# One Mamba-style decoder layer: powers behind other key chunks on GpSimd, squares summed with ones stationary, keys loaded ahead of weights

## The chip, the cores and the metric

The kernel runs on one core of one Trainium2 chip. The metric is the device time of one execution in microseconds, the median of several runs. A core has TensorE (PE, matmuls, with its weight loads listed apart as PEld), VectorE (DVE), ScalarE (ACT), GpSimd (POOL), and SyncE (SP), whose queue issues the DMAs.

## What is computed

The layer works on x of 8 batches x 128 positions x 512 channels in float32. Cut to what matters here:

```python
# 1: state-space mixer, 128 heads of 64, 8 groups of 16 heads
y = Y * silu(gate)                             # 8192 channels
gg = y.reshape(b, s, 8, 1024)
gg = gg * rsqrt(mean(gg * gg, axis=-1) + EPS)  # a root mean square of each group
x = layernorm(x + (gg * norm_w) @ out_proj_w.T)
# 2: attention over ctx: 32 query heads of 16, 8 key heads, 128 keys, no projections
x = layernorm(x + softmax(q @ k.T / 4 + mask) @ v)
# 3: feed-forward, 1792 hidden
x = layernorm(x + (silu(x @ Wg.T) * (x @ Wu.T)) @ Wd.T)
```

## The kernel before

All batches stay on chip. Each engine has its own program written out by hand, and semaphores tie them together: `wait_ge(S["name"], n)` holds an engine until the count is there, `then_inc` raises it.

**Mixer.** 64 tiles of 128 channels (two heads each; `TILES`), eight tiles a group (`TPG`), go through in 72 steps. For a tile, TensorE projects (lines 249 to 251: float32 as high and low parts in three matmuls of 512 columns), ScalarE and VectorE do convolution and decay, TensorE makes the head outputs (`outputs`, line 1216, into `ps_y`), VectorE combines and gates them (`combine`), and ScalarE copies them as `g_hi` (line 603) and squares them into `sq_tmp` (line 606). GpSimd adds the squares of the group's tiles into `sq_acc` (`add_square`). Output products (`out_products`, lines 1224 to 1226) are made of four tiles at a time (`TPH`).

**End of the mixer.** The last group has its own order. TensorE's part starts after the loop: `last_products` for batches 0 to 3 on the tiles that are ready, the outputs of tile 63, `earlier_squares` (sums of `sq_acc` over the 128 channels, eight matmuls with one moving column, line 1286), `last_squares` (the same for the two halves of `sq_tmp` of tile 63, line 1295), then the other products: batches 0 to 3 in `ps_hs` and `ps_gate`, 4 and 5 in `ps_dec`, 6 and 7 in `ps_gate` again. VectorE takes the two sums (lines 1010 and 1016), ScalarE the root, VectorE the reciprocal (line 816). Then for each batch VectorE adds the group's first half (`first_part`, line 810, two SBUF inputs) and its second half (`second_part`, line 1001, from PSUM), and takes the statistics of the first layernorm (`row_stats`, lines 968 and 970). Groups before the last sum their squares on another path (`square_sums`, `group_variance`: ones stationary, 512 columns, and the diagonal taken by a reduce against the identity, line 876).

**Attention.** 32 key chunks, four a batch. For chunk i GpSimd spreads the keys into a block-diagonal tile `k_bd` (line 506; two buffers, so it waits for the scores of chunk i-2), TensorE makes the scores (`scores`, line 1386, two matmuls of 64 rows), VectorE adds the mask and takes the minimum in eight reduces (`masked`, line 1048), ScalarE takes eight exponentials (line 715), TensorE turns the result (line 1396), ScalarE and VectorE each copy a half (`keep_turned`, lines 723 and 1057), and TensorE multiplies by the values (line 1410) and turns back. The layernorm's power -0.5 is taken by GpSimd (`powers`, lines 498 and 501) between two chunks. Its loop:

```python
for i in range(CHUNKS):
    need(pool, S["s_ps"], 2 * i - 2)
    gp.tensor_tensor(k_bd[i % 2][:, :, :],
...
    if i == 3:
        powers(1, slice(2, HB))
```

VectorE normalises (`normed`, line 986) batches 2 and 3 after the first powers, 4 to 7 after the second, and for the next stage 0 to 3 after the third, from chunk 23 on.

**Feed-forward.** It starts in the attention's last chunks, when batches 0 to 3 are ready (line 1439), and is a dense stream of matmuls.

**SyncE's queue** at the end of the mixer: mask, keys (`k_rep`, two loads from HBM, then six copies inside SBUF, line 346), values, then `w_gate` and `w_up` (lines 349, 350; 1.75 MB each), then `w_down` in tiles.

## Time and profile before

| what | us |
|---|---|
| median of 3 runs | 1640.75 |
| lowest, highest | 1639.96, 1640.96 |
| profiled execution: its own time | 1639.42 |
| profiled execution: span | 1637.7 |

| engine | busy us | share of the span | instructions |
|---|---|---|---|
| TensorE, matmuls | 1612.5 | 98% | 9120 |
| TensorE, weight loads | 1271.7 | 78% | 9120 |
| VectorE | 1193.1 | 73% | 2355 |
| GpSimd | 976.6 | 60% | 741 |
| ScalarE | 946.3 | 58% | 1578 |

The mixer takes the span to about 1366 us, the attention from there to about 1477, the feed-forward the rest. The shares are means over these three parts. An f32 matmul whose operands are not split by the program leaves two records in the trace, one for each pass.

### The profile page before, as it was taken

Reading aid. Unit: us, or ns where it says so; the run is one execution under the profiler, and the core shown is the slowest. Engines: PE = TensorE matmul, PEld = TensorE weight load, DVE = VectorE, ACT = ScalarE, POOL = GpSimd, SP = SyncE. Lnnn points to the kernel's source line nnn. Section 1 sums busy time; section 2 is a strip of 40 time slices with the busy share of each in tenths; the row PEclk is TensorE's granted clock in tenths of the full one; section 3 lists DMA queues with packets and bytes.
Section 4 is the critical chain, followed back from the end, with each engine's and each line's share of the span. In section 5 each row is a group of like instructions: output and inputs, shape, how many; then the busy total and the mean of one; then the engine's idle time right before and its main releaser. Section 6 shows DMA issues by size and latency. Waiting matters only on the chain.

```text
span 1637.7 us, 25607 instructions
## 1 busy us (share of the span) xinstructions
PE 1612.5 (98%) x9120; PEld 1271.7 (78%) x9120; DVE 1193.1 (73%) x2355; ACT 946.3 (58%) x1578; POOL 976.6 (60%) x741
## 2 busy tenths in 40 slices
PE   9999999999999999999999999999999998989998
PEld 7788888888888888888888888888888885544646
DVE  7767687767877686868685868586858689996433
ACT  6765377446745583648373837383738375985231
POOL 4977478656956694759484959385938573331000
PEclk9999999999999999999999999999999999999999
DMA  5422134213312241224231413141413254000000
GB/s 202 146 103 82 55 109 130 78 59 102 129 61 84 90 136 57 92 68 132 73 103 50 143 59 123 46 136 58 136 45 115 80 99 116 1 18 23 13 14 26
DMA packets 73571, 138.85 MB, mean 85 GB/s; under 512 B 6786, under 2 KB 10882, under 8 KB 73092
## 3 DMA queue, kind: packets, MB, share of 16 engines
q1 hardware_dynamic: 73444, 137.21, 26.5%
q8 instruction: 73, 1.20, 0.3%
q14 instruction: 54, 0.44, 0.1%
HBM read 132.98 MB, written 2.63 MB: 83 GB/s over the span
## 4 chain that ended last, share of the span: by engine, by line
PE 92%; DVE 4%; issue 1%; POOL 1%; DMA 1%; ACT 1%; SPq 0%; DVEq 0%; POOLq 0%; ACTq 0%
PE ps_hs L249 8%; PE ps_hs L251 8%; PE ps_hs L250 8%; PE ps_gate L250 8%; PE ps_gate L249 8%; PE ps_gate L251 8%; PE ps_y L1216 7%; PE ps_hs L1224 7%; PE ps_hs L1226 7%; PE ps_hs L1225 7%; PE ps_gate L1200 4%; PE ps_y L1514 3%; PE ps_hs L1439 3%; PE ps_dec L1439 3%; DVE pr L1048 2%
## 5 line engine op out<-in xcount | busy, mean ns | idle before, releaser
L798 DVE SCALAR_TENSOR_TENSOR conv<-ps_hs,cw,conv 128x508 f32<-128x508 f32 (+2 forms) x432 | 320.0, 741 | 31.6 <-ACT conv L565 20.4
L399 POOL TENSOR_TENSOR cum_bc<-cum_bc,neg_cum 128x1024 f32<-128x1024 f32 x128 | 247.4, 1932 | 10.8 <-POOL cum_bc L389 0.2
L249 PE MATMUL ps_hs<-x_hi,w_hi 128*128 128x512 f32 x576 | 231.3, 402 | 0.0
L251 PE MATMUL ps_hs<-x_hi,w_lo 128*128 128x512 f32 x576 | 225.1, 391 | 0.0
L249 PE MATMUL ps_gate<-x_hi,w_hi 128*128 128x512 f32 x576 | 224.2, 389 | 0.0
L250 PE MATMUL ps_hs<-x_lo,w_hi 128*128 128x512 f32 x576 | 224.2, 389 | 0.0
L250 PE MATMUL ps_gate<-x_lo,w_hi 128*128 128x512 f32 x576 | 224.1, 389 | 0.0
L251 PE MATMUL ps_gate<-x_hi,w_lo 128*128 128x512 f32 x576 | 224.0, 389 | 0.0
L1224 PE MATMUL ps_hs<-wo_hi,g_hi 128*128 128x512 f32 x488 | 190.4, 390 | 0.0
L1226 PE MATMUL ps_hs<-wo_hi,g_lo 128*128 128x512 f32 x488 | 190.2, 390 | 0.0
L1225 PE MATMUL ps_hs<-wo_lo,g_hi 128*128 128x512 f32 x488 | 190.1, 390 | 0.0
L833 DVE TENSOR_TENSOR m_sb<-ps_dec,cb 128x512 f32<-128x512 f32 x256 | 174.0, 680 | 12.7 <-ACT ps_dec L598 12.6
L603 ACT ACTIVATE g_hi<-ps_y 128x512 fp32r<-128x512 f32 x128 | 75.4, 589 | 178.9 <-DVE ps_y L845 178.7
L372 POOL TENSOR_TENSOR w_lo<-w_raw,w_hi 128x1024 fp32r<-128x1024 f32 (+1 forms) x72 | 172.2, 2392 | 8.1 <-ACT w_hi L529 2.4
L598 ACT ACT_TABLE_LOAD x64 | 82.1, 1283 | 160.3 <-DVE cb L805 159.3
L598 ACT ACTIVATE ps_dec<-cum_bc 128x512 f32<-128x512 f32 x256 | 149.5, 600 | 35.8 <-DVE m_sb L833 30.3
L389 POOL TENSOR_SCALAR_AFFINE_SELECT cum_bc<-cum_bc 128x1024 f32<-128x1024 f32 x128 | 140.5, 1098 | 31.7 <-DMA cum_bc<-cum_scratch 30.7
L565 ACT ACTIVATE conv<-ps_hs,cbias,cw 128x512 f32<-128x512 f32 x144 | 112.7, 783 | 65.6 <-PE ps_hs L251 65.5
L411 POOL TENSOR_TENSOR sq_acc<-sq_acc,sq_tmp 128x512 f32<-128x512 f32 x110 | 140.8, 1299 | 9.2 <-ACT sq_tmp L606 9.2
L841 DVE SCALAR_TENSOR_TENSOR ps_y<-hs,d_col,ps_y 128x512 f32<-128x512 f32 x128 | 95.9, 749 | 62.3 <-PE ps_y L1216 62.3
L469 POOL CAST wo_hi<-wo_sc 128x512 fp32r<-128x512 f32 x64 | 39.2, 612 | 152.8 <-PE ps_hs L1226 152.7
L1216 PEld LDWEIGHTS ps_y<-m_sb,xdt 128*64 128x64 f32 x2048 | 110.7, 137 | 25.1 <-issue 23.7
(176 smaller groups left out, 3334.2 us busy)
## 6 DMA issues: line engine op xcount, KB each, us to landing
cum_bc<-cum_scratch SPq DMA_DIRECT2D x128, 512.0 KB, 4.1
w_raw<-w_in SPq DMA_DIRECT2D x145, 256.0 KB, 4.6
wo_raw<-w_out SPq DMA_DIRECT2D x64, 256.0 KB, 5.0
g_acc<-x_t SPq DMA_DIRECT2D x4, 512.0 KB, 6.2
acc<-x_nat SPq DMA_DIRECT2D x1, 2048.0 KB, 9.7
out<-y_out SPq DMA_DIRECT2D x8, 256.0 KB, 2.0
wg_sb<-w_gate SPq DMA_DIRECT2D x1, 1792.0 KB, 13.6
wu_sb<-w_up SPq DMA_DIRECT2D x1, 1792.0 KB, 15.3
```

The source lines that it names most:

```text
L249: eng.matmul(ps, whi, xhi, start=(k == 0), stop=False)
L250: eng.matmul(ps, whi, xlo, start=False, stop=False)
L251: return eng.matmul(ps, wlo, xhi, start=False, stop=(k == n - 1))
L372: return gp.tensor_tensor(w_lo[slot][:, subs], w_raw[slot][:, subs], w_hi[slot][:, subs].bitcast(F32), ALU.subtract)
L399: gp.tensor_tensor(part, part, start.broadcast_to([P, 2, HB, SEQ]), ALU.add).then_inc(S["bc_ok"], 1)
L598: sc.activation(ps_dec[e][:, :], cum_bc[bh][:, e, :], ACT.Exp).then_inc(S["exp_ok"], 1)
L798: v.scalar_tensor_tensor(out=dst, in0=src, scalar=cw[:, at, TAPS - 1 - n:TAPS - n], in1=dst, op0=ALU.mult, op1=ALU.add).then_inc(S["tap"], 1)
L833: v.tensor_tensor(flat(m_sb[:, q]), ps_dec[q % 2][:, :], flat(half(cb, q // 2)), ALU.mult)\
L1216: mm = pe.matmul(ps_y[bh][e * HD:(e + 1) * HD, b * SEQ:(b + 1) * SEQ], xdt[:, bh * HB + b, e * HD:(e + 1) * HD], m_sb[:, 2 * bh + e, b, :] ...
L1224: pe.matmul(ps, g_hi[:, j, cols], wo_hi[:, j, :], start=(j == 0), stop=False)
L1225: pe.matmul(ps, g_hi[:, j, cols], wo_lo[:, j, :], start=False, stop=False)
L1226: return pe.matmul(ps, g_lo[:, j, cols], wo_hi[:, j, :], start=False, stop=(j == TPH - 1))
```

## The change

Three pieces. On GpSimd the three `powers` move behind later chunks of keys: from 3, 7 and 23 to 4, 9 and 25. In the last group the squares are summed with `ones` stationary and 512 squares moving, four matmuls that accumulate in the two `ps_dec` banks, in place of sixteen with one moving column; every row of a bank then holds all sums, and VectorE takes the diagonal in eight reduces against `ident`. The third matmul waits only for the first half of the squares of tile 63, and both groups now stand ahead of all products of tiles 62 and 63. SyncE waits for the six key copies ahead of the two feed-forward weights.

```diff
@@ SyncE
             sp.wait_ge(S["exp_ok"], 4 * TILES)
+            sp.wait_ge(S["k_in"], 16 * 2 * REP)
             sp.dma_start(wg_sb[:, :, :], w_gate).then_inc(S["wg_in"], 16)
@@ GpSimd
-                if i == 3:
+                if i == 4:
                     powers(1, slice(2, HB))
-                if i == 7:
+                if i == 9:
                     powers(1, slice(HB, BATCH))
-                if i == 23:
+                if i == 25:
                     powers(2, slice(0, HB))
@@ VectorE
-            dve.wait_ge(S["ss_early"], 1)
-            v.tensor_scalar(rstd_g[:, :], ps_dec[0][:, 0:BATCH], 1.0 / (TPG * P), EPS, ALU.mult, ALU.add)\
-                .then_inc(S["ss_part"], 1)
             dve.wait_ge(S["m3_in"], 16)
             v.tensor_scalar(mask_sb[:, :], mask_sb[:, :], -1.0, None, ALU.mult).then_inc(S["m3_neg"], 1)
-            dve.wait_ge(S["ss_part"], 1)
-            dve.wait_ge(S["ss_ps"], GROUPS)
-            v.scalar_tensor_tensor(out=rstd_g[:, :], in0=ps_y[0][:, 0:BATCH], scalar=1.0 / (TPG * P),
-                                   in1=rstd_g[:, :], op0=ALU.mult, op1=ALU.add).then_inc(S["rstd_v"], 1)
+            for b in range(BATCH):
+                cols = slice(b % HB * SEQ, (b % HB + 1) * SEQ)
+                if b % HB == 0:
+                    dve.wait_ge(S["ss_half"], b // HB + 1)
+                v.tensor_tensor_reduce(out=sq_tmp[:, b // HB, cols], in0=ps_dec[b // HB][:, cols], in1=ident[:, :],
+                                       scale=1.0, scalar=0.0, op0=ALU.mult, op1=ALU.add,
+                                       accum_out=rstd_g[:, b:b + 1]).then_inc(S["ss_diag"], 1)
+            dve.wait_ge(S["ss_diag"], BATCH * GROUPS)
+            v.tensor_scalar(rstd_g[:, :], rstd_g[:, :], 1.0 / (TPG * P), EPS, ALU.mult, ALU.add)\
+                .then_inc(S["rstd_v"], 1)
@@ TensorE
             def earlier_squares(t):
                 pe.wait_ge(S["sq_add"], 2 * t)
-                for b in range(BATCH):
-                    mm = pe.matmul(ps_dec[0][:, b:b + 1], sq_acc[:, b * SEQ:(b + 1) * SEQ], ones[:, 0:1],
-                                   start=True, stop=True)
-                mm.then_inc(S["ss_early"], 1)
+                pe.wait_ge(S["m_ok"], 4 * t + 4)
+                for h in range(2):
+                    pe.matmul(ps_dec[h][:, :], ones[:, :], sq_acc[:, h * HALF:(h + 1) * HALF], start=True, stop=False)
             def last_squares(t):
-                pe.wait_ge(S["sq_ok"], 2 * t + 2)
-                pe.wait_ge(S["g_lo_ok"], 2 * t + 1)
-                for b in range(BATCH):
-                    mm = pe.matmul(ps_y[0][:, b:b + 1],
-                                   sq_tmp[:, b // HB, (b % HB) * SEQ:(b % HB + 1) * SEQ], ones[:, 0:1],
-                                   start=True, stop=True)
-                mm.then_inc(S["ss_ps"], 1)
+                for h in range(2):
+                    pe.wait_ge(S["sq_ok"], 2 * t + h + 1)
+                    pe.matmul(ps_dec[h][:, :], ones[:, :], sq_tmp[:, h, :], start=False, stop=True)\
+                        .then_inc(S["ss_half"], 1)
...
             earlier_squares(t)
-            pe.wait_ge(S["wo_lo_ok"], t)
-            last_products((0,), (2,))
             last_squares(t)
             pe.wait_ge(S["wo_lo_ok"], t + 1)
-            last_products((0,), (3,))
+            pe.wait_ge(S["g_lo_ok"], 2 * t + 1)
+            last_products((0,), (2, 3))
             last_products((1,), (2, 3))
             last_products((2, 3), (2, 3))
             pe.wait_ge(S["g_lo_ok"], 2 * t + 2)
-            pe.wait_ge(S["ss_part"], 1)
+            pe.wait_ge(S["ss_diag"], BATCH * GROUPS)
             last_products((4, 5), range(TPH))
```

**TensorE, end of the mixer**, from the outputs of the last tile (in a name the stationary operand stands last); before:

```order
L1216 MATMUL ps_y<-m_sb,xdt 64x128 x7
L1286 MATMUL ps_dec<-ones,sq_acc 128x1 [waits sq_add]
L1286 MATMUL ps_dec<-ones,sq_acc 128x1 x7
L1224 MATMUL ps_hs<-wo_hi,g_hi 128x512 [waits wo_lo_ok]
L1225 MATMUL ps_hs<-wo_lo,g_hi 128x512
L1226 MATMUL ps_hs<-wo_hi,g_lo 128x512
L1295 MATMUL ps_y<-ones,sq_tmp 128x1 [waits g_lo_ok,sq_ok]
L1295 MATMUL ps_y<-ones,sq_tmp 128x1 x7
L1224 MATMUL ps_hs<-wo_hi,g_hi 128x512 [waits wo_lo_ok]
```

and now:

```order
L1220 MATMUL ps_y<-m_sb,xdt 64x128 x7
L1291 MATMUL ps_dec<-sq_acc,ones 128x512 [waits m_ok,sq_add]
L1291 MATMUL ps_dec<-sq_acc,ones 128x512
L1297 MATMUL ps_dec<-sq_tmp,ones 128x512 [waits sq_ok] x2
L1228 MATMUL ps_hs<-wo_hi,g_hi 128x512 [waits g_lo_ok,wo_lo_ok]
```

Sixteen matmuls have become four, and the three products that stood between the two groups stand behind them.

**GpSimd, the attention's loop**, from the values' copy to the third powers; before:

```order
L506 TENSOR_TENSOR k_bd<-k_rep,kbd_mask 128x512 [waits s_ps] x2
L498 TENSOR_SCALAR rstd<-mv 128x2 [waits mv1]
L501 TENSOR_TENSOR rstd<-rstd,minus_half 128x2 [waits eps1]
L506 TENSOR_TENSOR k_bd<-k_rep,kbd_mask 128x512 [waits s_ps] x4
L498 TENSOR_SCALAR rstd<-mv 128x4 [waits mv1]
L501 TENSOR_TENSOR rstd<-rstd,minus_half 128x4 [waits eps1]
L506 TENSOR_TENSOR k_bd<-k_rep,kbd_mask 128x512 [waits s_ps] x16
L498 TENSOR_SCALAR rstd<-mv 128x4 [waits mv2]
L501 TENSOR_TENSOR rstd<-rstd,minus_half 128x4 [waits eps2]
L506 TENSOR_TENSOR k_bd<-k_rep,kbd_mask 128x512 [waits s_ps] x8
```

and now:

```order
L507 TENSOR_TENSOR k_bd<-k_rep,kbd_mask 128x512 [waits s_ps] x3
L499 TENSOR_SCALAR rstd<-mv 128x2 [waits mv1]
L502 TENSOR_TENSOR rstd<-rstd,minus_half 128x2 [waits eps1]
L507 TENSOR_TENSOR k_bd<-k_rep,kbd_mask 128x512 [waits s_ps] x5
L499 TENSOR_SCALAR rstd<-mv 128x4 [waits mv1]
L502 TENSOR_TENSOR rstd<-rstd,minus_half 128x4 [waits eps1]
L507 TENSOR_TENSOR k_bd<-k_rep,kbd_mask 128x512 [waits s_ps] x16
L499 TENSOR_SCALAR rstd<-mv 128x4 [waits mv2]
L502 TENSOR_TENSOR rstd<-rstd,minus_half 128x4 [waits eps2]
L507 TENSOR_TENSOR k_bd<-k_rep,kbd_mask 128x512 [waits s_ps] x6
```

The powers stand one chunk later the first time, two chunks later the second and third time.

## Rows read from the trace of the kernel before

**Rows 1.** The page, part 1: busy time of the engines.

```profile
PE 1612.5 (98%) x9120; PEld 1271.7 (78%) x9120; DVE 1193.1 (73%) x2355; ACT 946.3 (58%) x1578; POOL 976.6 (60%) x741
```

**Rows 2.** Stretches: length, busy us of each engine, granted clock, DMA share.

```profile
core 0: us, PE busy (x) PEld busy (x) DVE busy (x) ACT busy (x) POOL busy (x), PEclk, DMA share, GB/s
...
1351.80:1355.30 3.50, 3.50 (x10) 2.73 (x9) 3.22 (x6) 0.00 (x0) 0.00 (x0) 0.51 1.35 159
...
1390.00:1441.00 51.00, 47.14 (x304) 24.96 (x300) 49.15 (x306) 50.91 (x157) 14.99 (x15) 1.00 0.01 2
...
1444.00:1448.00 4.00, 3.90 (x14) 1.00 (x15) 1.47 (x2) 0.00 (x0) 2.23 (x2) 0.57 0.00 0
```

**Rows 3.** Chain of waits, 1344 to 1373 us: start, us, what.

```profile
1346.02 1.88 PE ps_dec L1286 x16
...
1348.72 1.95 PE ps_y L1295 x16
...
1362.65 0.44 PE ps_y L1375 x4
...
1365.84 1.06 PE ps_hs L1386 x4
```

**Rows 4.** VectorE's timeline, 1349 to 1371 us: start, us, what, idle before.

```profile
1349.45 0.22 DVE L1013 TENSOR_SCALAR mask_sb<-mask_sb 128x128 f32<-128x128 f32 x1
1350.78 0.17 DVE L1016 SCALAR_TENSOR_TENSOR rstd_g<-ps_y,rstd_g 128x8 f32<-128x8 f32 x1 [1.11 <-PE ps_y L1295]
...
1362.28 1.53 DVE L810 SCALAR_TENSOR_TENSOR acc<-g_acc,rstd_g,acc 128x512 f32<-128x512 f32 x1
...
1364.57 1.40 DVE L810 SCALAR_TENSOR_TENSOR acc<-g_acc,rstd_g,acc 128x512 f32<-128x512 f32 x2
...
1367.07 0.29 DVE L1048 CUSTOM_DVE_ANT_0 pr<-ps_hs,mask_sb 128x128 f32<-128x128 f32 x1 [0.43 <-PE ps_hs L1386]
...
1369.90 0.75 DVE L1001 SCALAR_TENSOR_TENSOR acc<-ps_gate,rstd_g,acc 128x512 f32<-128x512 f32 x1 [1.90 <-PE ps_gate L1226]
```

**Rows 5.** GpSimd's timeline, 1355 to 1372 and 1428 to 1447 us.

```profile
1360.47 2.79 POOL L506 TENSOR_TENSOR k_bd<-k_rep,kbd_mask 128x512 f32<-128x512 f32 x2 [12.00 <-DMA k_rep<-k_rep]
1367.02 1.04 POOL L506 TENSOR_TENSOR k_bd<-k_rep,kbd_mask 128x512 f32<-128x512 f32 x1 [3.76 <-PE ps_hs L1386]
...
1441.65 0.23 POOL L498 TENSOR_SCALAR rstd<-mv 128x4 f32<-128x4 f32 x1 [8.17 <-DVE mv L970]
...
1442.96 2.23 POOL L506 TENSOR_TENSOR k_bd<-k_rep,kbd_mask 128x512 f32<-128x512 f32 x2
```

**Rows 6.** TensorE's timeline at the scores of chunks 8 and 24.

```profile
1389.54 1.13 PE L1386 MATMUL ps_hs<-k_bd,q_t 64*128 64x512 f32 x4 [1.09 <-POOL k_bd L506]
...
1444.10 2.08 PE L1386 MATMUL ps_hs<-k_bd,q_t 64*128 64x512 f32 x4 [4.47 <-POOL k_bd L506]
```

**Rows 7.** VectorE's timeline, 1436 to 1450 us; the first row closes chunk 22's masks.

```profile
1439.44 0.08 DVE L1048 DVE_READ_ACCUMULATOR2_ANT neg_max<- 128x1 f32 x1
...
1443.74 1.72 DVE L986 TENSOR_SCALAR acc<-acc,mv,rstd 128x512 f32<-128x512 f32 x2
1448.87 0.69 DVE L1057 COPY pr_t<-ps_gate 128x512 f32<-128x512 f32 x1 [3.40 <-PE ps_gate L1396]
```

**Rows 8.** ScalarE's timeline, 1438 to 1450 us.

```profile
1448.43 0.60 ACT L723 ACTIVATE pr_t<-ps_gate 128x512 f32<-128x512 f32 x1 [5.17 <-PE ps_gate L1396]
```

**Rows 9.** TensorE's timeline at one group of value products, and its second four.

```profile
1390.59 1.06 PE L1410 MATMUL ps_y<-pr_t,v_ext 128*32 128x512 f32 x8
...
1391.05 0.61 PE L1410 MATMUL ps_y<-pr_t,v_ext 128*32 128x512 f32 x4
```

**Rows 10.** VectorE's timeline, 1227 to 1230 us: the variance of an earlier group.

```profile
1227.17 0.28 DVE L876 CUSTOM_DVE_ANT_0 sq_tmp<-ps_y,ident 128x128 f32<-128x128 f32 x1
...
1228.97 1.28 DVE L880 TENSOR_SCALAR rstd_g<-rstd_g 128x8 f32<-128x8 f32 x1
```

**Rows 11.** ScalarE's exponentials, 1371 to 1390 and 1425 to 1441 us: min/median/max ns.

```profile
L715 ACT ACTIVATE pr<-pr,neg_max x45: 384/388/403, 1371.5 to 1389.8; 128x128 f32<-128x128 f32 x45
...
L715 ACT ACTIVATE pr<-pr,neg_max x41: 447/461/474, 1424.8 to 1440.7; 128x128 f32<-128x128 f32 x41
```

More of the change, by code:

```diff
@@ L209, in build @@
             "y_ps", "t_ok", "g_ok", "g_hi_ok", "g_lo_ok", "sq_ok", "sq_add", "wo_in0", "wo_in1", "wo_sc_ok", "wo_hi_ok", "wo_lo_ok",
-            "o_ps", "gacc_ok", "ss_ps", "sqs_hi", "sqs_lo", "ss_diag", "half_ok", "ss_early", "ss_part", "rstd_v", "rstd_root", "rstd_inv", "acc_ok",
+            "o_ps", "gacc_ok", "ss_ps", "sqs_hi", "sqs_lo", "ss_diag", "half_ok", "ss_half", "rstd_v", "rstd_root", "rstd_inv", "acc_ok",
             "k_in", "v_in", "m3_in", "m3_neg", "v_zero", "v_ones", "v_ok", "kbd_m", "kbd_ok",
```

## Prediction

> **What bounds the kernel now.** The page comes first: TensorE is busy for 98% of the span [rows 1], so nearly the whole program is a stream of matmuls, and a small change has to be looked for where that stream is slow or stands still. The view by stretches shows two places after 1340 us where the granted clock is at half (1.2 instead of 2.4 GHz): 0.51 in 1351.8 to 1355.3 us, and 0.57 in 1444 to 1448 us; between them it is 1.00 [rows 2]. Both lie next to a part of the change.
>
> The chain of waits names the work ahead of the first. After the last head outputs, TensorE sums the squares in two groups of eight matmuls with one moving column each, 1.88 and 1.95 us, mostly weight loads. Then matmuls of 512 columns, 45 of them, run until 1362.65 us, the slow stretch among them [rows 3]. Up to 1369.9 us the chain is TensorE; then it goes to VectorE, whose timeline shows how much room it had until then: idle 0.43 us before the first score mask and 1.90 us before `second_part(7)`, 2.3 in all [rows 4]. From there the attention loop of 32 key chunks begins. In it VectorE has almost no gaps, so that what VectorE gains or loses, the end gains or loses: TensorE's feed-forward part, dense to the end, starts when VectorE has masked chunk 31.
>
> The largest hole is at chunk 24. GpSimd has built the keys of chunk 23, then takes up `powers(2)`, which waits 8.17 us for VectorE's statistics of batch 3; only at 1442.96 us does it build chunk 24 [rows 5]. TensorE wants that chunk: its scores start at 1444.10 after 4.47 us of waiting, and last 2.08 us at the half clock instead of 1.13 [rows 6]. VectorE then stands 3.40 us [rows 7], ScalarE 5.17 us [rows 8]. At chunk 8 the same pattern costs TensorE 1.09 us [rows 6].
>
> **Part 1, sums of squares on TensorE.** Removed are 3.83 us (1.88 and 1.95). Added are four f32 matmuls, ones against 512 moving columns. The nearest rows are the value products: eight records, which begin as two rounds of four, the second 0.46 us after the first [rows 9]. I read a round as one pass side by side in the array, so a full f32 matmul is two passes, 0.92 us. The upper bound is the pair of score matmuls, 1.06 us [rows 3]; if that pair ran one after the other, the lower bound is 0.53. I take 0.92, since the value products show the pass itself: 3.7 us, 0.15 saved, and 0.1 more as one switch between kinds goes. The last half needs ScalarE's last square, before which the old group could not start either (1348.72); the new third matmul ends at 1348.8, so nothing waits.
>
> The clock is worth more. With 512 columns the array streams, where one column left it nearly empty, so I expect no fall: the 3.5 us at 0.51 give back 0.49 x 3.5 = 1.7 us. TensorE thus comes to the last batch 1.9 us earlier (bounds: without the clock's part, 0.3 less at 1.06 a matmul, so about -0.3; with it and 0.53 a matmul, 3.5).
>
> **Part 2, the diagonal on VectorE.** Two instructions on 8 columns become eight reduces and one scale. The group variance of earlier groups is the same code: from the first reduce, 1227.17, to the scale, 1228.97, is 1.80 us [rows 10]. VectorE has negated the mask by 1349.6 [rows 4], the first half's sums are there, the second half's come at 1349.7 and are wanted at 1350.4. The scale begins at 1351.4 where the old one began at 1350.78 [rows 4]: VectorE starts on the last group 0.6 us later. Root and reciprocal follow as before. The bank's next use, batch 4, waits for all reduces: TensorE is there at 1355 (1349.7 and 24 matmuls of 0.23 us), and the reduces are done since 1351.4, so nothing.
>
> To this comes a collision. GpSimd builds chunk 2 once the scores of chunk 0 are out, at 1367.02 [rows 5], while VectorE does masks, which do not suffer. With scores 1.9 us earlier it runs at 1365.1 to 1366.1, upon two `first_part` steps (1.40 us for two, [rows 4]). What such an overlap costs is on record: the `first_part` at 1362.28 lasts 1.53 us where its neighbours take 0.70, beside GpSimd's first two chunks [rows 4, 5]. I count 0.7.
>
> So VectorE is free for the masks at 1366.6 + 0.6 + 0.7 = 1367.9, and with 0.93 for four of them reaches `second_part(7)` at 1368.9, later than TensorE delivers (1368.0). Against 1369.90 the gain is **1.0 us**; without the collision it would be 1.7. The page SBUF — State Buffer of the Trainium skill (Who interferes with whom) says why one kind suffers: the shared port pair is an exclusive lock, and a VectorE instruction with two SBUF inputs contends for it, one with a single SBUF input outside the 2-port modes doesn't. By that rule the new reduces, which read PSUM and the identity, cost the same beside GpSimd, and the sum would stay.
>
> **Part 3, keys ahead of the weights.** GpSimd starts chunk 0 at 1360.47 and has it ready by about 1362 [rows 5], TensorE asks for it at 1365.84 [rows 3], now 1363.9: two us of room with no change at all. Earlier keys gain nothing there, and only shift GpSimd's first two overlaps. The weights leave some us later; their first use is the feed-forward part, over 100 us on. Zero; if the overlap falls on one more VectorE step, 0.7 lost (in the range).
>
> **Part 4, powers moved.** Chunk 24's keys need only the scores of chunk 22, long out; they are built ahead of `powers(2)`, as is chunk 25, which needs the scores of 23 (out before VectorE ends chunk 22). So scores 24 start when VectorE has masked chunk 22, at 1439.5 [rows 7], not at 1444.1; the idle time and the half clock go. The powers still start when the statistics come (1441.65) and end at 1443.0, before VectorE uses them at 1443.74, so no new wait. Now late next is VectorE itself: it works through two normalisations, 1.72 us with GpSimd beside them [rows 7], and goes straight on. The gain is its 3.40 us, and up to 0.5 of the overlap, since GpSimd's keys lie beside the normalisations only until 1444.0 (one chunk behind the powers, 1.04 us) instead of 1445.2 (two, 2.23 us, [rows 5]): **3.7 us** (3.4 to 3.9). ScalarE ends chunk 22 at 1443.3 (1448.43 less its idle 5.17, [rows 8]) and keeps ahead. At chunk 8 the 1.09 us end at 1389.54; VectorE's masks of chunk 6, which those scores also need, are done only a few tenths before, so most of the wait would stay under another name: **0.2** (0 to 1.0). Moving the first powers from chunk 3 to 4 costs nothing: they are used two masks later.
>
> **Sum.** 1.0 + 0 + 3.7 + 0.2 = 4.9 us. The profiled execution took 1639.42 us (span 1637.7), which gives 1634.5; the median of the runs is 1640.75, 1.3 higher, which gives **1635.8 us**.
>
> **Rivals.**
> *The clock falls after the projection all the same.* If the granted level follows something else, such as the short waits around 1348, 1.7 us stay. TensorE gains 0.3, VectorE has room to follow: 0.3 + 3.9 = 4.2, so 1636.5. For it: the fall came only at 1351.8, when full matmuls were already running. Chance 0.12.
> *ScalarE takes over the loop.* Its exponentials lengthen in the unbroken stretch, from a median of 388 ns before 1390 to 461 ns after 1425 [rows 11], and the pause at chunk 24 comes just then. If that is a real slowing, eight more chunks at 8 x 0.07 us lose 4.5 of what is gained, which leaves at most about 1: 1639.8, no change. Against it: VectorE's pace holds through the same stretch, and after the pause it has gaps nowhere. Chance 0.15.
> *The clock falls in the attention loop, slower than before.* A third of its matmuls are transposes; with other timing the array may count as idle. Each fall costs some 1.6 us as at 1351.8, so more than three eat the gain and six give 1645.5. Against it: 1.00 in all of 1390 to 1441 with the same mixture [rows 2]. Chance 0.06. TensorE: Matmul & The Clock Gate of the Trainium skill (Part 4: PE-mode transpose) has a sentence that speaks for this: a transpose does not count as a busy array in the same way. By that rule falls would already be spread over the loop; this trace shows one, after 4.1 us without any matmul.
> *More than forecast:* no collision, and chunk 8's whole wait gone: 1.7 + 3.9 + 1.0 = 6.6, 1634.1. Chance 0.05. The forecast itself: 0.62.
>
> **Numbers.** Outside 0.2% (3.3 us) a measurement of this kernel can tell a change. Faster by more: the forecast, the first rival and the last, less some of each where two terms come out small, 0.76; within: 0.18; slower: 0.06. The range goes from 7.0 us gained (1.9, 1.0 and 3.9 together with a little) to 2.7 (a small gain ahead of the loop and 3.4 less a new wait): 1633.7 to 1638.1.
>
> **What would show it.** Right: granted clock 1.00 from 1346 to 1480; four matmuls of about 0.9 us; the scale 0.6 us later relative to the last squares; VectorE with no idle time above 1 us from 1367 to 1475; scores 24 within 0.3 us of the masks of chunk 22. Wrong: a half-clock stretch anywhere in these, a VectorE wait on TensorE or on the powers at chunk 24, or ScalarE's records still growing while VectorE waits.

## The result and the profile after

| | before | after |
|---|---|---|
| median, us | 1640.86 (6 runs) | 1633.28 (6 runs) |
| lowest to highest | 1639.96 to 1643.47 | 1632.67 to 1634.53 |
| profiled execution: time, span | 1639.42, 1637.7 | 1632.67, 1630.9 |

The ratio is 0.995, with a 95% interval of 0.9939 to 0.9961: 7.6 us faster. Forecast were 1635.8 us and a range down to 1633.7, so the change does more than the range allowed, by 0.4 us. That excess is smaller than the spread of the runs; the 2.5 us between forecast and median are not. The two profiled spans are 6.8 us apart.

The first view is the page's busy time, which answers to [rows 1]. VectorE's sum is 0.9 us smaller though it has eight reduces more; the rows below show steps of it that have become shorter.

```profile
PE 1609.1 (99%) x9096; PEld 1268.2 (78%) x9096; DVE 1192.2 (73%) x2370; ACT 945.8 (58%) x1578; POOL 975.8 (60%) x741
```

TensorE by stretches, against [rows 2] (length, its busy time, granted clock, DMA share, GB/s): both half-clock stretches are gone, and the clock is at its upper level from the squares to the end of the loop.

```profile
core 0: us, PE busy (x), PEclk, DMA share, GB/s
1346.00:1351.80 5.80, 5.80 (x20) 1.00 1.02 116
1351.80:1355.30 3.50, 3.50 (x17) 1.00 1.14 122
1390.00:1441.00 51.00, 48.30 (x310) 1.00 0.00 1
1444.00:1448.00 4.00, 2.85 (x19) 1.00 0.00 0
```

The chain of waits, against [rows 3]. The last head outputs, the four square matmuls (two records each, so 0.96 us a matmul), the turned queries (the transposes of x for the attention's queries), the scores:

```profile
1344.49 1.02 PE ps_y L1220 x16
1345.51 1.91 PE ps_dec L1291 x4
1347.43 1.92 PE ps_dec L1297 x4
...
1360.28 0.44 PE ps_y L1374 x4
...
1363.46 1.06 PE ps_hs L1385 x4
```

The head outputs already start 0.5 us earlier than in the profiled execution before, which the change does not touch; what follows is therefore counted from the start of those outputs. Behind them TensorE has shortened by 1.9 us. VectorE's timeline, against [rows 4]:

```profile
1350.82 0.17 DVE L1020 TENSOR_SCALAR rstd_g<-rstd_g 128x8 f32<-128x8 f32 x1
...
1362.39 0.74 DVE L811 SCALAR_TENSOR_TENSOR acc<-g_acc,rstd_g,acc 128x512 f32<-128x512 f32 x1
...
1363.91 1.41 DVE L811 SCALAR_TENSOR_TENSOR acc<-g_acc,rstd_g,acc 128x512 f32<-128x512 f32 x2
...
1367.52 0.75 DVE L1002 SCALAR_TENSOR_TENSOR acc<-ps_gate,rstd_g,acc 128x512 f32<-128x512 f32 x1 [0.70 <-PE ps_gate L1230]
```

The scale is 0.04 us later on the clock, so 0.54 later once the 0.5 us are taken off. But no `first_part` is lengthened by more than 0.07 us, neither the one at 1362.39 (1.53 us before) nor the pair, and VectorE comes to `second_part(7)` 0.70 us before TensorE. GpSimd's timeline, against [rows 5], shows who waited instead: chunk 2 takes 1.58 us, not 1.04. Its last two rows are at chunk 24:

```profile
1359.58 2.49 POOL L507 TENSOR_TENSOR k_bd<-k_rep,kbd_mask 128x512 f32<-128x512 f32 x2 [11.57 <-DMA k_rep<-k_rep]
1364.64 1.58 POOL L507 TENSOR_TENSOR k_bd<-k_rep,kbd_mask 128x512 f32<-128x512 f32 x1 [2.57 <-PE ps_hs L1385]
...
1439.12 0.23 POOL L499 TENSOR_SCALAR rstd<-mv 128x4 f32<-128x4 f32 x1 [1.88 <-DVE mv L971]
...
1440.43 1.04 POOL L507 TENSOR_TENSOR k_bd<-k_rep,kbd_mask 128x512 f32<-128x512 f32 x1
```

TensorE's scores of chunks 8 and 24, against [rows 6]. Chunk 8 still waits 0.94 us, now for VectorE's masks; chunk 24 waits no more:

```profile
1387.01 1.13 PE L1385 MATMUL ps_hs<-k_bd,q_t 64*128 64x512 f32 x4 [0.94 <-DVE neg_max L1052]
...
1437.15 1.13 PE L1385 MATMUL ps_hs<-k_bd,q_t 64*128 64x512 f32 x4
```

And VectorE at the same place, against [rows 7]. The two normalisations take 1.00 us instead of 1.72 and the turned probabilities follow at once:

```profile
1441.22 1.00 DVE L987 TENSOR_SCALAR acc<-acc,mv,rstd 128x512 f32<-128x512 f32 x2
1442.13 0.68 DVE L1061 COPY pr_t<-ps_gate 128x512 f32<-128x512 f32 x1
```

ScalarE's exponentials, against [rows 11], grouped over 1371 to 1390, 1422 to 1437 and 1441 to 1470 us (busy us, mean ns of one). The records lengthen up to 1444 us and are short again behind a pause of 0.90 us at 1445.88, as they were behind the 5.17 us of the kernel before:

```profile
L716 ACT ACTIVATE pr<-pr,neg_max 128x128 f32<-128x128 f32 x48 | 14.7, 390 | 0.0
```

```profile
L716 ACT ACTIVATE pr<-pr,neg_max 128x128 f32<-128x128 f32 x38 | 12.4, 448 | 0.0
```

```profile
L716 ACT ACTIVATE pr<-pr,neg_max 128x128 f32<-128x128 f32 x64 | 20.1, 400 | 0.0
```

What lengthens is each record, not the work: from one exponential to the next it is 0.29 us in all three stretches, in both kernels. Eight of them in a row take 2.44 us at 1376.80 and 2.51 at 1438.21, where each record is 0.08 us longer:

```profile
1376.80 2.44 ACT L716 ACTIVATE pr<-pr,neg_max 128x128 f32<-128x128 f32 x8
...
1438.21 2.51 ACT L716 ACTIVATE pr<-pr,neg_max 128x128 f32<-128x128 f32 x8
```

### The profile page after: what moved, and what is told of

It is laid out like the page before. It is cut to its first block, busy times and chain, and to the rows that moved or that the text cites. A ratio compares the mean times of both kernels' runs of the same rounds, so it can differ in the third digit from the quotient of the medians.

```text
span 1630.9 us, 25574 instructions
## 1 busy us (share of the span) xinstructions
PE 1609.1 (99%) x9096; PEld 1268.2 (78%) x9096; DVE 1192.2 (73%) x2370; ACT 945.8 (58%) x1578; POOL 975.8 (60%) x741
## 3 DMA queue, kind: packets, MB, share of 16 engines
q8 instruction: 72, 1.18, 0.3%
## 4 chain that ended last, share of the span: by engine, by line
PE 92%; DVE 5%; issue 1%; DMA 1%; ACT 0%; POOL 0%; SPq 0%; DVEq 0%; POOLq 0%; ACTq 0%
PE ps_hs L249 8%; PE ps_hs L251 8%; PE ps_hs L250 8%; PE ps_gate L250 8%; PE ps_gate L249 8%; PE ps_gate L251 8%; PE ps_y L1220 7%; PE ps_hs L1229 7%; PE ps_hs L1230 7%; PE ps_hs L1228 7%; PE ps_gate L1204 4%; PE ps_y L1513 3%; PE ps_hs L1438 3%; PE ps_dec L1438 3%; DVE pr L1052 2%
```

## How the profiles are compared

Every profile splits at two rows: the start of the last head outputs (TensorE), and `second_part(7)` (VectorE), behind which the loop begins. A is the time from the one to the other, B from `second_part(7)` to the end of the span. What happens ahead of A differs by a microsecond or more between executions and says nothing of the edit. Times are medians; the ratio column has the 95% interval of the ratio to the kernel before run beside them. B is good to about 0.05 us, since it is taken from a span that is given to 0.1.

| kernel | median us | ratio | start | A | B |
|---|---|---|---|---|---|
| before | 1640.86 | | 1344.92 | 24.98 | 267.80 |
| powers only | 1636.51 | 0.9958 to 0.998 | 1344.83 | 26.55 | 263.42 |
| powers 3, 7, 25 | 1636.54 | 0.9957 to 0.998 | 1344.25 | 24.95 | 263.60 |
| squares only | 1638.81 | 0.9978 to 0.9996 | 1344.32 | 23.89 | 267.59 |
| keys only | 1641.96 | 0.9996 to 1.0013 | 1345.81 | 26.57 | 268.92 |
| all but keys | 1633.77 | 0.9948 to 0.9973 | 1344.75 | 23.60 | 263.35 |
| powers and keys | 1635.35 | 0.9956 to 0.9981 | 1345.48 | 26.58 | 263.44 |
| the same, groups adjacent | 1636.18 | 0.9961 to 0.9982 | 1345.26 | 25.62 | 263.62 |
| the same, spread | 1635.99 | 0.9958 to 0.9981 | 1345.61 | 25.22 | 263.37 |
| all (after) | 1633.28 | 0.9939 to 0.9961 | 1344.42 | 23.10 | 263.38 |
| all, again | 1633.69 | 0.9945 to 0.9973 | 1343.92 | 23.11 | 263.37 |
| all but keys, fenced | 1633.23 | 0.994 to 0.9967 | 1345.37 | 23.11 | 263.42 |
| all, squares fp32r | 1633.62 | 0.9943 to 0.9968 | 1344.49 | 23.04 | 264.17 |
| the same, reordered | 1632.14 | 0.9936 to 0.9961 | 1344.90 | 22.16 | 264.04 |

The kernel before had medians of 1641.23, 1640.83 and 1641.26 beside the three groups of runs.

## Experiments: the parts alone

**Powers alone**, at 4, 9 and 25, and only the last of them moved:

```diff
-                if i == 23:
+                if i == 25:
                     powers(2, slice(0, HB))
```

> Only the three powers moved behind chunks 4, 9 and 25; squares and keys as before. Theory A (each part is worth what its own wait was): 4.3 us faster than the kernel before, from the second score matmul on: VectorE goes straight from the two normalisations of chunk 23 to the copy of chunk 24, the half clock at chunk 24 is gone, the one at the end of the mixer stays. Theory B (ScalarE takes over the loop, part of the gain came from the squares): under 2.5 us.

> Only the third powers moved, from chunk 23 to 25. Theory A: the same 4.2 us as all three, since chunk 8's wait is followed by one on VectorE's masks. If the first two matter: 1 us less than with all three.

Both are 4.7 us faster than the kernel before beside them. B falls by 4.4 us from the profile before in the first and by 4.2 in the second: what moving the first two powers adds is 0.2 us in B and nothing in the medians. A stays where it was in the second; that it is 1.6 us longer in the first, in a stretch that the edit does not touch, was not expected, and is taken up below.

**Keys alone**: only SyncE's wait for the six key copies ahead of the weights.

> Only the keys ahead of the weights. Theory A: no change within 0.5 us, since the last second_part waits for TensorE; GpSimd starts chunk 0 up to 1 us earlier. Theory C: VectorE's stalled first_part (1.53 us) gets short, which shows in its timeline, and the time does not move because VectorE had idle time behind it.

1641.96 against 1641.23, an interval that holds 1: nothing. Its profile, span 1641.3, had both A and B longer than before, by 1.6 and 1.1 us, which is taken up below. The lengthened `first_part` of theory C is short there (0.75 us), but that is no proof for the keys: two of the three further profiles of the unchanged kernel below have none lengthened either.

**Squares alone**: the change without its keys and powers.

> Only the squares changed (ones stationary, diagonal on VectorE); powers and keys as before. Theory A: 1.9 us faster, 1.65 of it the granted clock, which stays at 1.00 from 1346 to 1362 us; from the end of the last head outputs to the last second_part 22.0 us instead of 23.9. Theory C (the missing collision on VectorE came from the earlier keys): a first_part lasts about 1.5 us again, and the gain is 1.0 us.

2.4 us faster in the median. A is 23.89, 1.09 us under the profile before, which is the 1.0 of the prediction, and as predicted both overlaps are on VectorE (1.53 and 2.26 us), as theory C has it. So the forecast's picture holds in this profile, of a kernel without the early keys; in the changed kernel A is 0.8 us shorter still.

## Experiments: who stands when GpSimd and VectorE meet

The changed kernel again, and the changed kernel without its early keys:

```diff
-            sp.wait_ge(S["k_in"], 16 * 2 * REP)
             sp.dma_start(wg_sb[:, :, :], w_gate).then_inc(S["wg_in"], 16)
```

> The changed kernel once more, beside the three below, so that they have it from the same chip and hour. All theories: 1633.3 us within 0.6. In the profile TensorE starts the queries of batch 0 15.7 us after the last head outputs begin, granted clock 1.00 in all of 1335 to 1480.

> The changed kernel without its early keys (the weights are again issued ahead of them). Theory A (once the squares are short, VectorE is the bound at second_part(7), and earlier keys let GpSimd start its chunk 0 some 0.9 us sooner, so that GpSimd and not VectorE stands in their overlaps): 0.8 us slower than the changed kernel, 1634.1, with VectorE's first_part at 1.5 us and a pair at 2.2, and second_part(7) 23.9 us after the last head outputs begin instead of 23.1. Theory B (the keys are worth nothing, the 0.8 us between two profiles was chance): within 0.3 of the changed kernel, and second_part(7) at 23.1.

A came out again to 0.01 us. Without early keys it is 0.5 us longer in its profile, not 0.8, and the medians (1633.77 and 1633.69) cannot tell them apart. GpSimd's chunk 0 starts 0.5 us later there, not 0.9. VectorE's timeline of the kernel without early keys, then GpSimd's:

```profile
1360.68 1.32 DVE L810 SCALAR_TENSOR_TENSOR acc<-g_acc,rstd_g,acc 128x512 f32<-128x512 f32 x1
...
1364.74 2.19 DVE L810 SCALAR_TENSOR_TENSOR acc<-g_acc,rstd_g,acc 128x512 f32<-128x512 f32 x2
...
1368.35 0.74 DVE L1001 SCALAR_TENSOR_TENSOR acc<-ps_gate,rstd_g,acc 128x512 f32<-128x512 f32 x1
```

```profile
1364.96 1.42 POOL L506 TENSOR_TENSOR k_bd<-k_rep,kbd_mask 128x512 f32<-128x512 f32 x1 [2.06 <-PE ps_hs L1384]
```

Chunk 2 arrives 0.22 us after the pair has begun, waits out the first step, and gets in ahead of the second: the pair loses 0.8 us, and VectorE reaches `second_part(7)` with no room left. In the changed kernel it arrives 0.73 us after, when the second step has just begun, and waits itself. Half a microsecond decides which engine pays, and it is VectorE that was shifted: TensorE's scores release chunk 2 20.2 us after the last head outputs begin in both kernels, while the pair begins at 19.5 us in the changed kernel and at 20.0 in this one. The delay came from chunk 0. It starts 15.16 us after those outputs in the changed kernel, and the `first_part` at 15.9 loses 0.07 us; here it starts at 15.66, and that step takes 1.32 us instead of 0.74.

How far the early keys are what moves chunk 0 is less clear. With them it starts 14.98 to 15.37 us after the outputs in seven profiles and at 16.22 in an eighth (the adjacent groups, below); without them, 15.26 to 16.13 in nine. The median of the six key copies, from issue to landing, is 8.7 us before and 8.5 after. To take the meeting away, chunk 2 was fenced, that is, held until VectorE has done its last `first_part`:

```diff
             for i in range(CHUNKS):
                 need(pool, S["s_ps"], 2 * i - 2)
+                if i == 2:
+                    pool.wait_ge(S["acc_ok"], BATCH * GROUPS)
```

> The changed kernel without early keys, as the run before it without them, but GpSimd builds chunk 2 only when VectorE has done its last first_part. Theory A (VectorE's two first_part steps of 2.19 us in that kernel are lengthened by GpSimd's chunk 2, which got in between them; nothing else makes them long): the pair lasts 1.41 us, second_part(7) starts 23.1 us after the last head outputs begin (22.9, then held by TensorE) where it was 23.6, chunk 2 lasts 1.04, and the loop behind it is unchanged. The single first_part beside chunk 0 stays at 1.32. Theory B (the length has another cause, the weights' transfers for one): the pair stays at 2.19. Time: A 1633.3, B 1633.8; the times alone can hardly tell them.

```profile
1364.96 1.40 DVE L812 SCALAR_TENSOR_TENSOR acc<-g_acc,rstd_g,acc 128x512 f32<-128x512 f32 x2
...
1368.48 0.75 DVE L1003 SCALAR_TENSOR_TENSOR acc<-ps_gate,rstd_g,acc 128x512 f32<-128x512 f32 x1 [0.62 <-PE ps_gate L1231]
```

```profile
1366.51 1.04 POOL L508 TENSOR_TENSOR k_bd<-k_rep,kbd_mask 128x512 f32<-128x512 f32 x1 [3.40 <-DVE acc L812]
```

As theory A had it: pair 1.40, chunk 1.04, A 23.11, without the early keys and with the transfers under way as in the unfenced kernel (DMA share 1.02 from 1364 to 1367 us in both), so those do not lengthen the pair. One thing was not as expected: chunk 0 started at 15.26 us in this execution, and the single `first_part` beside it took 0.90 us, not 1.32. The pair therefore began at 19.6 us, and without the fence chunk 2, which in three kernels with these matmuls came at 20.2 us, would have come just as the second step began. So this profile shows that the pair is short when nothing meets it, but not how much the fence itself saved. What early keys can be worth in A is a meeting avoided; that they avoid it in most executions is not shown, and no median shows it.

## Experiments: what holds the clock

Powers and keys as changed, squares as before the change; then with the two one-column groups next to each other, in the changed kernel's place; then with one product behind each of the sixteen:

```diff
+            for b in range(BATCH):
+                mm = pe.matmul(ps_dec[0][:, b:b + 1], sq_acc[:, b * SEQ:(b + 1) * SEQ], ones[:, 0:1],
+                               start=True, stop=True)
...
+                product(b)
...
+            for b in range(BATCH):
+                mm = pe.matmul(ps_y[0][:, b:b + 1],
+                               sq_tmp[:, b // HB, (b % HB) * SEQ:(b % HB + 1) * SEQ], ones[:, 0:1],
+                               start=True, stop=True)
...
+                product(BATCH + b)
```

> Powers and early keys as in the changed kernel, the squares still in sixteen one-column matmuls. Theory A (the squares are worth 1.9 to 3.5 us of TensorE's time there, by how deep the clock falls in an execution, of which VectorE passes on what it can follow): slower than the changed kernel by 2.5 to 3.5, 1636.2, with a stretch of granted clock at 0.5 after the projection and turned queries 17.5 to 19.2 us after the last head outputs begin. Theory B (squares gain only their own 0.2 us and the fall comes whatever is there): within 0.7 of the changed kernel, 1633.9.

> As the one before, but both groups of one-column sums stand next to each other, in the changed kernel's place, with its order of the last products. Theory A (the one-column form is what lets the clock fall): the fall stays, 0.5 in about 3.5 us, and the time is that of the kernel before it in this list within 0.6, 1636.4 (a little more, since the last group waits for the square with nothing between: 0.3). Theory B (the order, or the gap between the groups, is what made it fall): granted clock 1.00 and turned queries at 15.9, time within 0.8 of the changed kernel.

> Powers and early keys as in the changed kernel, squares in one-column matmuls as before the change, but each of the sixteen is followed by one 512-column product that anyway has to be done, so that no two stand together. Theory A (what drops the clock is a stretch of some 1.9 us or more that is nearly all weight loads): granted clock 1.00 in all of 1346 to 1362, and the turned queries of batch 0 come 16 to 17 us after the last head outputs begin, against 18.2 to 19.2 in the kernels with groups. VectorE gets its sums about 1.8 us later, so the time may be no better than theirs: 1635.5. Theory B (one-column matmuls drop it wherever they stand, by their share over a longer stretch): a stretch at 0.5 stays, 18 us or more, 1637.

Stretches of TensorE in the three, in this order (length, busy time, granted clock, DMA share, GB/s):

```profile
1350.00:1354.00 4.00, 4.00 (x16) 0.50 1.17 139
1354.00:1357.00 3.00, 3.00 (x9) 0.53 0.96 104
```

```profile
1350.00:1354.00 4.00, 4.00 (x16) 0.58 0.85 107
```

```profile
1350.00:1354.00 4.00, 4.00 (x29) 1.00 1.17 139
1354.00:1357.00 3.00, 3.00 (x15) 1.00 0.94 98
```

The fall goes with groups of one-column matmuls, wherever the groups stand, and is absent when each such matmul has a 512-column product behind it. The spread form still costs: VectorE has its scale at 1353.93, 8.3 us after the last head outputs begin, against 6.4 in the changed kernel, and TensorE waits 0.93 us at the turned queries. In A it lies between the changed kernel and the groups (25.22), with VectorE and not TensorE reaching `second_part(7)` last, and in the median it gains nothing on the groups. The adjacent form lost time differently from forecast: TensorE stood 0.83 us for the last squares, not 0.3. Against the changed kernel (1633.69) the groups cost 1.7 and 2.5 us in the median, where 2.5 to 3.5 was expected of the first.

## Experiments: is the fall the same each time?

The kernel before, profiled three times more, nothing edited.

> The kernel before, profiled once more. Theory A (the half-clock stretch after the projection has no fixed place: it lasts as long in some executions as in others but begins earlier or later, and covers more or less of the dense stream): from the start of the last head outputs to the turned queries of batch 0 it takes 17.55 us or 19.15 us, as in the profiles of the kernels with one-column groups so far, and the span follows: 1637.7 with the first, 1639.3 with the second. From second_part(7) to the end 267.6 to 268.9 us, by the same play at chunk 24. Theory B (the kernel before always has 17.55, and what made 19.15 was the edit in the others): 17.55 again.

> As the one before, a second look: A 17.55 or 19.15, B 17.55.

> As the one before, a third look: A at least one of the three looks at 19.15 or near it, B none.

| profile | start | A | B | span |
|---|---|---|---|---|
| first | 1344.58 | 26.53 | 267.89 | 1639.0 |
| second | 1344.39 | 26.57 | 267.84 | 1638.8 |
| third | 1348.39 | 24.95 | 269.06 | 1642.4 |

Stretches of TensorE in the first, and VectorE's row at chunk 24 in the third ([rows 7] had 3.40):

```profile
1350.00:1354.00 4.00, 4.00 (x11) 0.50 0.71 90
1354.00:1357.00 3.00, 3.00 (x9) 0.55 1.07 120
1444.00:1448.00 4.00, 2.70 (x8) 0.68 0.00 0
```

```profile
1453.43 0.69 DVE L1057 COPY pr_t<-ps_gate 128x512 f32<-128x512 f32 x1 [4.51 <-PE ps_gate L1396]
```

Theory B falls; theory A holds in its numbers. Read in slices of 1 us, the half clock after the projection lasted 6.8 us in the first two profiles and 3.4 in the third, as in the profile of before; A is 1.6 us longer where it is the 6.8. At chunk 24 it is the other way round: 3.4 us in the first two, over 6 in the third, and B is 1.2 us longer there. Powers alone, keys alone, and powers and keys together had the 6.8 after the projection, the adjacent groups 3.4. So what sets the cost is the length of the fall, which differs by a factor of two, where theory A had named its place. The place differs as well: the long falls begin 4.0 to 5.3 us after the last head outputs, the short ones 5.4 to 7.1. B of the third is 0.2 us above what was expected. Not forecast was the third profile's start, 3.5 us late; the clock was at 0.98 in its first 100 us, far ahead of the change. The first two missed the 1639.3 of the expectation by 0.3 and 0.5 us, since they start earlier.

The meeting of VectorE and GpSimd differs between these profiles too. The `first_part` that took 1.53 us in the profile before took 0.74 in the second and third, and in the first another one, 15.7 us after the outputs, took 1.55.

## Experiments: a version beyond both

In the changed kernel TensorE holds `second_part(7)` by 0.7 us. The four square matmuls take 3.83 us because their operands are f32. Here GpSimd and ScalarE write the last group's squares as fp32r, into tiles that are free by then (the sums are of squares rounded to that type):

```diff
-                gp.tensor_tensor(part, part, sq_tmp[:, bh, :], ALU.add).then_inc(S["sq_add"], 1)
+                total = part
+                if t == TILES - 2:
+                    pool.wait_ge(S["gate_ps"], 2 * STEPS)
+                    total = w_hi[0].rearrange("p a k c -> p (a k c)")[:, bh * HALF:(bh + 1) * HALF]
+                gp.tensor_tensor(total, part, sq_tmp[:, bh, :], ALU.add).then_inc(S["sq_add"], 1)
...
-                pe.matmul(ps_dec[h][:, :], ones[:, :], sq_tmp[:, h, :], start=False, stop=True)\
-                        .then_inc(S["ss_half"], 1)
...
+                pe.matmul(ps_dec[h][:, :], ones_r[:, :],
+                          w_hi[1].rearrange("p a k c -> p (a k c)")[:, h * HALF:(h + 1) * HALF],
+                          start=False, stop=True).then_inc(S["ss_half"], 1)
```

> The changed kernel with the last group's squares written as fp32r by the engines that make them, so that the four matmuls of 512 columns are of the one-pass kind. Theory A (the 0.96 us of one such f32 matmul is price of the type): 0.23 us each, TensorE 2.9 us shorter there, granted clock still 1.00. Then VectorE is the bound at second_part(7), 0.7 us earlier: 1632.6. Theory B (the clock was held by the long f32 passes and falls now): a stretch at 0.5 appears and the time is 1633.5 or more.

```profile
1345.51 0.73 PE L1299 MATMUL ps_dec<-w_hi,ones_r 128*128 128x512 f32 x2
...
1348.29 0.50 PE L1311 MATMUL ps_dec<-w_hi,ones_r 128*128 128x512 f32 x1 [1.46 <-ACT w_hi L615]
```

```profile
1363.91 2.19 DVE L819 SCALAR_TENSOR_TENSOR acc<-g_acc,rstd_g,acc 128x512 f32<-128x512 f32 x2
```

No gain: A 23.04, B 0.8 longer. TensorE now waits 1.46 us for the last square and, with the rest of the saving kept, asks for the scores so early that GpSimd's chunk 2 meets the pair at the wrong moment again: 2.19 us. At the sums and up to 1371 us the clock stays at 1.00, so there it was not the long f32 matmuls that held it. But it falls just behind, at the first chunks of the attention, where the changed kernel has no fall. The same two stretches in this kernel, in the second version below, and in the changed kernel:

```profile
1367.00:1371.00 4.00, 2.65 (x12) 1.00 0.88 364
1371.00:1376.00 5.00, 4.26 (x16) 0.66 0.01 4
```

```profile
1367.00:1371.00 4.00, 2.21 (x12) 1.00 0.93 387
1371.00:1376.00 5.00, 4.73 (x17) 0.66 0.03 11
```

```profile
1367.00:1371.00 4.00, 3.26 (x15) 1.00 0.88 364
1371.00:1376.00 5.00, 3.93 (x23) 1.00 0.00 1
```

The half clock lasts 3.4 us from 1371.8. VectorE then waits 0.66 us for the turned probabilities at 1375.56, where the changed kernel has no wait, and that is most of what B lost. Theory B's two signs, a stretch at 0.5 and 1633.5 us or more (1633.62), thus both came, though the stretch is not at the sums. What the records show ahead of it is a TensorE with more idle time, 2.65 us busy of the 4 us up to 1371 against 3.26; whether that is the reason was not tested. The second version puts products into the wait, takes the first four diagonals ahead of VectorE's last `g_low`, and fences chunk 2:

```diff
             g_low(TILES - 1, 0)
-            g_low(TILES - 1, 1)
...
+                if b == HB:
+                    g_low(TILES - 1, 1)
...
-            last_squares(t)
+            pe.wait_ge(S["wo_lo_ok"], t)
+            last_products((0,), (2,))
+            last_square(t, 0)
+            last_products((1, 2), (2,))
+            last_square(t, 1)
```

> As the one before, and VectorE takes the first half's four diagonals ahead of its last g_low, in a stretch where it is idle for 0.63 us, with the first half's sums served by TensorE between products; GpSimd's chunk 2 waits for the last first_part. Theory A (VectorE bounds second_part(7) from here on, and what it gains before the last group it gains there): the scale 0.6 us earlier, second_part(7) 1.3 us earlier than in the changed kernel: 1632.0, a version faster than both. Theory B (TensorE or the keys' arrival holds it): at most the 0.7 of the run before.

```profile
1360.39 1.10 DVE L821 SCALAR_TENSOR_TENSOR acc<-g_acc,rstd_g,acc 128x512 f32<-128x512 f32 x1
...
1367.06 0.74 DVE L1011 SCALAR_TENSOR_TENSOR acc<-ps_gate,rstd_g,acc 128x512 f32<-128x512 f32 x1
...
1374.92 0.69 DVE L1072 COPY pr_t<-ps_gate 128x512 f32<-128x512 f32 x1 [0.50 <-PE ps_gate L1416]
```

A is 22.16, 0.9 shorter (1.3 forecast; 0.36 went to the meeting with chunks 0 and 1, which has no fence). B is 0.66 longer: the clock fell here too, for 3.4 us from 1371.7, and VectorE has a new idle time of 0.50 us at 1374.92, where the changed kernel has none. In the profile 0.3 us of gain remain. The median, 1632.14 (1631.31 to 1633.91), is the lowest of all and 1.1 to 1.6 us under the five others of the changed kernel's kind, but the runs overlap; that it beats the changed kernel is likely, not settled.

## Why the prediction was off, step by step

**Squares on TensorE: right.** Forecast 3.7 us for the four, measured 3.83 (0.96 a matmul, not 0.92). From the head outputs to the turned queries TensorE went from 17.57 to 15.70 us, 1.9 as forecast: 1.7 of it is the clock (3.4 us at half). The four take as long as the sixteen did, so the 0.15 counted for them was nothing, and the other 0.2 would be the switch between kinds of matmul. Each of the two records of such an f32 matmul lasts 0.48 us, twice the 0.23 from one product to the next, so a record is not simply one pass of a product's kind. The rival that the clock falls after the projection all the same is false: 1.00 there in all five profiles with 512-column f32 sums, and in the two with fp32r, where it falls later.

**Diagonal: right.** 0.54 us later, 0.6 forecast.

**The collision: wrong.** "I count 0.7", for VectorE, "as such an overlap costs". The step took the engine that stands from one row of before, and carried VectorE's loss of 0.8 us at 1362.28 along in its 1366.6 as if it were fixed. The rows show that the one who comes second stands, on either engine, and that nothing is lost without a meeting. With the 0.8 kept, the pair begins at 20.2 us after the last head outputs, together with chunk 2, and VectorE stands: so it came out in the squares alone. Without it, as in the changed kernel, the pair begins at 19.5 us, the second step is ahead of chunk 2, and GpSimd stands. Both of VectorE's losses went, it had 0.70 us of room, and A gained all of TensorE's 1.88 us, not 1.0, against the profile before. Whether the 0.8 is there differs from execution to execution of the unchanged kernel, so that this went the good way in both profiles of the changed kernel is in part luck. Part 3 was priced at zero because TensorE does not need the keys earlier; what they move is chunk 0 against VectorE, worth 0.5 us in one pair of profiles and nothing that a median shows. The range had a further loss for the keys, and "more than forecast" counted one overlap avoided, not two. The Trainium skill (SBUF — State Buffer, Who interferes with whom) has the port pair as an exclusive lock, and these rows agree, 1.04 against 1.58 us on GpSimd and 1.40 against 2.19 on VectorE; the rule was read as if VectorE always lost.

**Powers: right mechanism, a little small.** B fell by 4.4 us from profile to profile against 3.9 forecast (3.7 and 0.2). The masks of chunk 22 end at 1437.0, the scores start at 1437.15. (Before, TensorE stood 4.47 us there, not the 4.1 of the prediction's rivals.) VectorE's normalisations took 1.00 for 1.72, so ending most of the overlap was worth 0.7, not up to 0.5: the one chunk behind the powers is over 0.25 us after they begin (1440.43 and 1.04), as forecast. Chunk 8: the wait stayed under another name, as forecast, 0.2 us.

**The sum's base: wrong.** "The profile gives 1634.5; the median is 1.3 higher." The step carries a profile's gain over to the median as if both half-clock stretches cost the same in every execution. They do not: in the eight profiles with the two groups of one-column sums where they were (before and its three further profiles, the two of the powers, keys, powers and keys), A is 24.95 to 24.98 in three and 26.53 to 26.58 in five, 25.96 in the mean. B of the five of them that have the stop at chunk 24 is 267.80 to 269.06, 268.3 in the mean. After, the two profiles agree (A 23.10 and 23.11, B 263.4 twice). By means, 25.96 - 23.10 = 2.9 and 268.3 - 263.4 = 4.9, together 7.8 us; the medians show 7.6. The profiled execution of before was a mild one at both places. Of the 2.9 us by which 7.8 exceeds the forecast of 4.9, the collision is 0.9 and the powers 0.5; 1.0 in A and 0.5 in B are this step.

**ScalarE takes over the loop: false.** The rival read the length of a record as the engine's pace. The records lengthened to 468 ns at 1441 us and were at 390 behind the next pause, but an exponential began every 0.29 us throughout, before and after. VectorE's idle times in the loop are 0.59 and 0.41 us, both at chunks 8 and 9, and one of 1.18 us at 1473.57, which the kernel before has as well (1.19 at 1480.32) and which the prediction's sign of "no idle time above 1 us" had overlooked. Why the records lengthen is open.

**Clock in the loop: false.** 1.00 throughout in the changed kernel; that a fall can come there is shown by the two fp32r kernels at 1371.7. Transposes are not a third of the matmul records in the loop but over half, 176 of 304 from 1390 to 1441 us before. The sentence of TensorE: Matmul & The Clock Gate in the Trainium skill on transposes (Part 4: PE-mode transpose) would have had falls here; no stretch from 1390 to 1441 us shows one, before or after.

## What to carry to other kernels

A stretch at half clock has no fixed price: profile the unchanged kernel several times before a gain is counted from it, and expect the spread to go with the fall. A loss where two engines meet need not be there in every execution either. When two engines meet at a shared resource, don't charge the engine that lost in the profile, but ask which will come second after the change, and fence the one that has room. After an edit, read the clock beyond the place that was edited: a gain in one stretch can let it fall in the next. Measure a kernel in pieces between two rows that every version has; here that told apart 0.5 us where medians could not tell 1.

## What was not expected of the hardware

- Groups of one-column f32 matmuls went with a half-clock stretch of 3.4 us in some executions and of 6.8 us in others of the same kernel, and so did the stop at chunk 24. Sixteen such matmuls each followed by a 512-column product show none.
- One f32 matmul of 128x512 takes 0.96 us in a row of them, two records. In fp32r the two that follow each other lie within 0.73 us, start to modelled end. With them the clock fell later, 3.4 us from 1371.7, in both kernels that had them.
- GpSimd's 128x512 product takes 1.04 us alone and up to 1.58 when VectorE's step with two SBUF operands is under way; VectorE's pair takes 1.40 alone and 2.19 to 2.26 when GpSimd gets in between.
- ScalarE's exponential records lengthen from 390 to 468 ns in an unbroken stretch while one still begins every 0.29 us.
